# Graph layers on one core: the leading run's repair by an adding scatter, and the second graph's one-hots against numbers kept in PSUM

## The chip, the cores and the metric

The kernel runs on one core of one Trainium2 chip. The metric is the device time of one execution in microseconds. Before the change the median of three runs is 8366.63 us (8365.44 to 8374.06). The core's engines are TensorE (PE), VectorE (DVE), ScalarE (ACT), GpSimd (POOL) and SyncE (SP). They run side by side and wait for each other on semaphores. SP and ACT issue plain DMAs. POOL issues the indirect ones, which fetch or write one row for each of 128 partitions, by an index read from SBUF.

## The reference

`x` holds 12500 nodes of 256 features. A first graph has 200000 edges, sorted by target. After a layer norm, three graph layers run over it:

```python
h = x @ W
msg = h[src] * norm[:, None]
out = jax.ops.segment_sum(msg, dst, num_segments=n_nodes)
return out + b            # gelu after the first two layers
```

The result is added to `x` and normed again. It is the input of an attention over a second graph (131072 unsorted edges) that scores four experts for each node, and of four feed-forward experts that the scores mix. The second graph needs its edges sorted by target and, for each target, the number of its edges.

## The kernel before

**Running sums instead of a scatter.** The first graph's sorted edges are laid out as 128 partitions by 1564 columns, each partition holding a stretch of consecutive edges. For each column POOL issues one gather (L995, in the tail L1005) that fetches the 128 source rows of 1 KB from `feature_table` in HBM. DVE adds the row to a running sum that starts anew where the target changes (L1130, one `scalar_tensor_tensor` for each column, state in PSUM). ACT copies four columns at a time from PSUM to SBUF (L915). SP writes 16 columns at a time to `running_features_of_edges` in HBM (L1229). A batch of 16 columns lives in one of four buffers, so POOL may be up to four batches ahead of DVE. A batch is added only when all its 16 rows of gathers have landed. There are 97.75 batches in a layer. The sum of a node is then the row of its last edge, which POOL fetches at the end of the layer, 98 gathers (L1024). DVE, PE and ACT apply the weight, the bias and the gelu to these, and SP writes the table of the next layer.

**The leading run.** A node's edges may begin in one partition's stretch and end in the next's. Then the row of its last edge in the later partition lacks the earlier partition's part. PE makes these parts in one product (`carry_from` by the last columns' sums, L1042) into `ps[:, 0, 0:D]`. After all of a layer's sums are in HBM (`s_out`), POOL gathers the 128 rows at `fix_at` into `run_fix` (L1012), DVE adds PE's part to them (L1140) into `run_fixed`, and POOL writes them back to the same rows (L1016), waits for that write and starts the 98 gathers of L1024. Partitions with nothing to repair point at spare rows. This happens three times, once in each layer.

**The second graph's work is woven into layer 0.** `SecondGraph.on_vector` is a generator. In layer 0, DVE takes one step of it (up to the next `yield`) after every fourth column; 1564 columns give 391 such slots, four in a batch. First come a few preparing steps, then the 64 steps that build one-hots, then some 167 steps of a bitonic sort (exchanges at L202 and L203, sign flips at L239, transposes on PE between them), then some 20 of bookkeeping. Steps left over after the last column run at the layer's end (`for _ in between: pass`).

A one-hot step `h` builds, for 16 edges of each partition, `lo` (128 numbers by 16 edges, L377) and `hi` (98 by 16, L379): the low seven bits and the upper bits of the target, compared with the numbers 0 to 127. The numbers stand in `iota_rep` in SBUF, each repeated 16 times, in bf16. Both are `tensor_tensor` with all operands in SBUF in bf16, in one slot. PE multiplies `lo` by `hi`, 16 matmuls (L195) into `ps[:, 5, 0:98]`, which counts each node's edges. The tiles are double-buffered (`s_hot`, `s_used`). In layer 0 the running sums use PSUM banks 0 to 3, the count bank 5, and the sort's transposes banks 4 to 7, after the count.

After the layers come the attention's 1024 gathers (L1454) beside the experts' matmuls (L1539, L1550), and the mix.

Of the kernel before, what the change touches and what calls it, by code (L numbers as in the profile page):

```python
# [5 lines left out]
ALU = mybir.AluOpType  # L6
# [6 lines left out]
P = 128  # L13
U = 16
# [22 lines left out]
def build(nc, x, src, dst, gnn_w, gnn_b, w_gat, att_src, att_dst, b_gat, ln_gamma, ln_beta,  # L37
          ew1, eb1, ew2, eb2, edges2, out):
    N, D = x.shape
    NB = -(-N // P)  # L40
# [24 lines left out]
    sums_dram = nc.dram_tensor("running_features_of_edges", (E1P + 2 * P, D), F32).ap()  # L65
# [5 lines left out]
    with ExitStack() as ctx:  # L71
        def sb(name, shape, dt=F32):
            return ctx.enter_context(nc.sbuf_tensor(name, shape, dt))
# [3 lines left out]
        def sem(name):  # L77
            s = nc.alloc_semaphore(name=name)
            phase_sems.append(s)
            return s  # L80
# [12 lines left out]
        ps = ctx.enter_context(nc.psum_tensor("ps", [P, 8, 512], F32))  # L93
# [12 lines left out]
        fix_at = sb("row_of_leading_run", [P, 1], I32)  # L106
# [56 lines left out]
        iota_rep = work[:, 0:P * U // 2].bitcast(BF16).rearrange("p (m u) -> p m u", u=U)  # L163
# [3 lines left out]
        def hot_tiles(rows):  # L167

            lo = [hot_bf[0:rows, a].rearrange("p (m u) -> p m u", u=U) for a in range(2)]
            hi = [hot_bf[0:rows, 2 + a, 0:NB * U].rearrange("p (m u) -> p m u", u=U) for a in range(2)]  # L170
            return lo, hi
# [116 lines left out]
        class SecondGraph:  # L288
# [56 lines left out]
            def on_vector(self, dve):  # L345

                C = COLS2
                link = Chain(dve, self.s_d)
# [20 lines left out]
                yield  # L369
                link(nc.vector.tensor_scalar(self.keys[0].bitcast(I32), src_i, KEY_BASE, None, ALU.bitwise_or))  # L370
                lo, hi = hot_tiles(P)
                dve.sem_inc(self.s_used, 2)
                for h in range(C // U):
                    yield
                    dve.wait_ge(self.s_used, h + 1)
                    at = slice(h * U, (h + 1) * U)
                    nc.vector.tensor_tensor(lo[h % 2], iota_rep[0:P],  # L377
                                            lo16[:, at].unsqueeze(1).broadcast_to([P, P, U]), ALU.is_equal)
                    nc.vector.tensor_tensor(hi[h % 2], iota_rep[0:P, 0:NB],  # L379
                                            hi16[:, at].unsqueeze(1).broadcast_to([P, NB, U]),  # L380
                                            ALU.is_equal).then_inc(self.s_hot, 1)
                yield
# [454 lines left out]
        state = [ps[:, k // 2, (k % 2) * D:(k % 2 + 1) * D] for k in range(U)]  # L837
        spare = onehot[:].rearrange("p a u m -> p (a u m)")
        selfs = spare[:, 0:4 * 2 * D].rearrange("p (r a f) -> p r a f", r=4, a=2)
        run_fix, run_fixed = spare[:, 8 * D:9 * D], spare[:, 9 * D:10 * D]  # L840
        sums_rows = sums_dram[0:E1P].rearrange("(p c) f -> p c f", p=P)

        pairs4 = [work[:, j * 8 * D:(j + 1) * 8 * D].rearrange("p (r a f) -> p r a f", r=4, a=2) for j in range(4)]
# [17 lines left out]

        s_row = [ctx.enter_context(nc.semaphore(f"rows_in{r}")) for r in range(4)]
        s_sums = [ctx.enter_context(nc.semaphore(f"node_sums_in{r}")) for r in range(4)]
        s_fixin, s_fixout = ctx.enter_context(nc.semaphore("gnn_fix_rows_in")), ctx.enter_context(nc.semaphore("gnn_fix_rows_out"))

        def layer(l, s_stored=None):

# [13 lines left out]
            s_carry, s_fixd = sem("carries" + n_), sem("fix_done" + n_)  # L881
# [102 lines left out]
            def on_gpsimd(pool):  # L984
                pool.sem_inc(s_c, 4 * U)
                if s_stored is not None:
                    pool.wait_ge(s_stored, 16 * PAIRS)

                def gather(m, r):
                    pool.wait_ge(s_stg, m + 1)  # L990
                    pool.sem_inc(s_tick, 1)
                    pool.wait_ge(s_c, m * U + (U + 1))
                    pool.sem_inc(s_tick, 1)
                    for k in range(U):
                        nc.gpsimd.indirect_dma_start(  # L995
                            out=rows_in[r][:, k], out_offset=None, in_=table,
                            in_offset=bass.IndirectOffsetOnAxis(ap=staged[:, r, k:k + 1], axis=0),
                        ).then_inc(s_row[r], 16)
                with pool.Fori(0, LAPS) as g:
                    for r in range(4):  # L1000
                        gather(g * 4 + r, r)
                for m, r, uses, size, c in tails:
                    pool.wait_ge(s_c, m * U + (U + 1))
                    for k in range(size):
                        nc.gpsimd.indirect_dma_start(  # L1005
                            out=rows_in[r][:, k], out_offset=None, in_=table,
                            in_offset=bass.IndirectOffsetOnAxis(ap=idx[0][:, c + k:c + k + 1], axis=0),
                        ).then_inc(s_row[r], 16)

                for r in range(S):  # L1010
                    pool.wait_ge(s_out[r], chunks_out[r])
                nc.gpsimd.indirect_dma_start(  # L1012
                    out=run_fix, out_offset=None, in_=sums_dram,
                    in_offset=bass.IndirectOffsetOnAxis(ap=fix_at[:, 0:1], axis=0)).then_inc(s_fixin, 16)
                pool.wait_ge(s_fixd, 1)
                nc.gpsimd.indirect_dma_start(  # L1016
                    out=sums_dram, out_offset=bass.IndirectOffsetOnAxis(ap=fix_at[:, 0:1], axis=0),
                    in_=run_fixed, in_offset=None).then_inc(s_fixout, 16)
                pool.wait_ge(s_fixout, 16 * (l + 1))
                for n in range(PAIRS):  # L1020
                    if n >= 4:
                        pool.wait_ge(s_sums[n % 4], node_base[n % 4] + 32 * (n // 4))
                    for b in (2 * n, 2 * n + 1):
                        nc.gpsimd.indirect_dma_start(  # L1024
                            out=acc[:, b * D:(b + 1) * D], out_offset=None, in_=sums_dram,
                            in_offset=bass.IndirectOffsetOnAxis(ap=take1[:, b:b + 1], axis=0)).then_inc(s_sums[n % 4], 16)
                if last:
                    for n in range(PAIRS):
                        pool.wait_ge(s_hc, n + 3)
                        for b in (2 * n, 2 * n + 1):  # L1030
                            nc.gpsimd.indirect_dma_start(  # L1031
                                out=first_dram, out_offset=bass.IndirectOffsetOnAxis(ap=put_at[:, b:b + 1], axis=0),
                                in_=HG[:, b, CH:GW], in_offset=None).then_inc(s_put, 16)
# [74 lines left out]
            def on_vector(dve):  # L1108
                if last:
                    link = Chain(dve, s_lk)  # L1110
# [25 lines left out]
                for _ in between:  # L1136
                    pass
                dve.wait_ge(s_carry, 1)
                dve.wait_ge(s_fixin, 16 * (l + 1))
                nc.vector.tensor_tensor(run_fixed, ps[:, 0, 0:D], run_fix, ALU.add).then_inc(s_fixd, 1)  # L1140

                if last:
                    dve.sem_inc(s_v, 2)
# [77 lines left out]
            def on_sync(sp):  # L1221
# [65 lines left out]
                if l == 0:  # L1287
                    sp.wait_ge(second.s_z, 32)
            return (on_scalar, on_gpsimd, on_tensor, on_vector, on_sync, s_o) + ((s_go,) if last else ())

        first = layer(0)
        after = layer(1, first[5])
        with nc.Block() as block:
# [21 lines left out]
            def _(sp):  # L1315
                first[4](sp)
                after[4](sp)
        end_phase()
        on_scalar, on_gpsimd, on_tensor, on_vector, on_sync, s_x1out, s_go = layer(2)


# [16 lines left out]
        def area(*shape):  # L1338
# [83 lines left out]
        s_tail, s_tailt, s_ende, s_endt, s_fixd, s_fixe, s_fixo = (sem(c) for c in (  # L1422
            "tails_ready", "tails_turned", "ends_scores", "ends_exps", "ends_turned", "fix_scores", "fix_exps"))
# [17 lines left out]
        with nc.Block() as block:  # L1441
# [236 lines left out]
            @block.vector  # L1678
            def _(dve):
                on_vector(dve)  # L1680
                link = Chain(dve, s_c)
                dve.wait_ge(s_x1out, 16 * PAIRS)
# [258 lines left out]
```

## Time and profile before

| | us |
|---|---|
| median of the runs | 8366.63 |
| the profiled execution | 8364.74 |
| its span | 8362.9 |
| POOL busy | 6097.1 (73%) |
| DVE busy | 3651.4 (44%) |
| PE busy | 2172.5 (26%) |
| ACT busy | 1974.1 (24%) |

Busy time counts an engine's own instructions. A POOL gather is busy for about 0.95 us and followed by 0.30 us that the profile calls issue, so an engine that gathers all the time shows about 76%. Layer 0 ends at 2228.9, layer 1 at 4346.4 and layer 2 at 6473.0 (each time the start of the first gather at L1024); the rest lasts until 8362.9.

### The profile page before, as it was taken

The numbers are of one execution on the slowest core, as the hardware profiler recorded it, in microseconds if no ns is written. First come the engines' busy times: TensorE is split into PE (matmuls) and PEld (weight loads), VectorE is DVE, ScalarE is ACT, GpSimd is POOL, SyncE is SP. The second block draws the span as 40 slices with busy tenths as digits, with TensorE's granted clock in tenths as the row PEclk, the third lists the DMA queues.
The fourth block names the chain that finished last, engine by engine and source line by source line (L and its number), as shares of the span: only waits on it lengthen the run. The fifth ranks groups of instructions, "written<-read, shape, count | busy, mean of one in ns | idle before, by whom it ended". The sixth has DMA issues, their size and how long they took to land. (4 is left out here: it accounts for less than half of the span.)

```text
span 8362.9 us, 48755 instructions
## 1 busy us (share of the span) xinstructions
PE 2172.5 (26%) x10310; PEld 1843.9 (22%) x10310; DVE 3651.4 (44%) x7508; ACT 1974.1 (24%) x3168; POOL 6097.1 (73%) x6330
## 2 busy tenths in 40 slices
PE   1440000000220000000013000000000899999974
PEld 1330000000220000000013000000000788888863
DVE  5676666443444333343434434343433723322346
ACT  1111212122332222221224212121221422222222
POOL 5777777777677777777766777777776777777761
PEclk9999999999965555555557555555555999999987
DMA  5555555566666666666666666666666943323348
GB/s 168 187 191 203 205 204 204 204 210 210 231 211 208 212 205 215 205 215 206 213 217 214 215 206 214 206 212 208 210 211 214 281 109 74 81 74 74 74 121 249
DMA packets 590695, 1583.16 MB, mean 189 GB/s; under 512 B 136696, under 2 KB 377188, under 8 KB 551780
## 3 DMA queue, kind: packets, MB, share of 16 engines
q1 hardware_dynamic: 307092, 896.86, 29.4%
q0 software_dynamic: 281888, 669.59, 27.9%
q10 hardware_dynamic: 1584, 15.48, 0.5%
q14 instruction: 113, 0.93, 0.0%
q8 instruction: 18, 0.29, 0.0%
HBM read 820.50 MB, written 760.96 MB: 189 GB/s over the span
## 5 line engine op out<-in xcount | busy, mean ns | idle before, releaser
L995 POOL DMA_INDIRECT acc<-feature_table,staged_indices x4608 | 4415.7, 958 | 1466.3 <-issue 1365.3
L1130 DVE SCALAR_TENSOR_TENSOR ps<-ps,keep_within_node,acc 128x256 f32<-128x256 f32 x4692 | 2310.1, 492 | 3296.4 <-DMA acc<-feature_table,staged_indices 2770.8
L915 ACT COPY acc<-ps 128x1024 f32<-128x1024 f32 x787 | 796.9, 1013 | 3215.9 <-DVE ps L1130 3215.9
L1454 POOL DMA_INDIRECT acc<-attention_table,idx x1024 | 1009.4, 986 | 312.0 <-issue 311.7
L1042 PE MATMUL ps<-work,carry_from_partition 128*128 128x256 f32 x4 | 2.4, 713 | 3948.6 <-ACT work L915 3948.6
L1042 PEld LDWEIGHTS ps<-work,carry_from_partition 128*128 128x128 f32 x4 | 1.0, 312 | 3949.4 <-ACT work L915 3949.4
L915 ACT COPY work<-ps 128x1024 f32<-128x1024 f32 x386 | 390.7, 1012 | 1522.8 <-DVE ps L1130 1522.8
L1539 PE MATMUL ps<-work 128*128 128x256 f32 x3136 | 703.5, 380 | 9.0 <-ACT work L1602 8.7
L1550 PE MATMUL ps<-work,onehot 128*128 128x256 f32 x3136 | 702.9, 380 | 9.9 <-DMA work<-L_ffn_W_in 9.9
L1539 PEld LDWEIGHTS ps<-work 128*128 128x128 f32 x3136 | 597.2, 191 | 91.6 <-ACT work L1602 10.1
L1550 PEld LDWEIGHTS ps<-work,onehot 128*128 128x128 f32 x3136 | 596.9, 190 | 91.5 <-issue 10.0
L1602 ACT ACTIVATE work<-ps,eb_sb 128x256 f32<-128x256 f32 x784 | 307.6, 475 | 997.2 <-PE ps L1550 994.5
L1695 DVE TENSOR_TENSOR acc<-ps,acc 128x512 f32<-128x512 f32 x196 | 135.6, 692 | 910.5 <-PE ps L1539 910.1
L1024 POOL DMA_INDIRECT acc<-unning_features_of_edges,last_edge_of_gnn_node x294 | 292.7, 996 | 93.8 <-issue 88.7
L195 PE MATMUL ps<-onehot 128*128 128x98 bf16 x1120 | 219.4, 366 | 201.1 <-DVE onehot L379 197.5
L283 PE MATMUL ps<-ident,work 128*128 128x128 f32 x112 | 27.6, 427 | 782.7 <-DVEq L253 782.7
L195 PEld LDWEIGHTS ps<-onehot 128*128 128x128 bf16 x1120 | 158.9, 148 | 261.4 <-DVE onehot L379 222.2
L283 PEld LDWEIGHTS ps<-ident,work 128*128 128x128 f32 x112 | 21.9, 223 | 788.1 <-DVEq L253 788.1
L1102 PE MATMUL ps<-gw_sb,work 128*128 128x256 f32 x784 | 189.6, 386 | 0.0
L1042 PE MATMUL ps<-acc,carry_from_partition 128*128 128x256 f32 x2 | 1.2, 712 | 695.5 <-ACT acc L915 695.5
L1042 PEld LDWEIGHTS ps<-acc,carry_from_partition 128*128 128x128 f32 x2 | 0.5, 313 | 695.8 <-ACT acc L915 695.8
L1102 PEld LDWEIGHTS ps<-gw_sb,work 128*128 128x128 f32 x784 | 143.7, 193 | 18.0 <-issue 0.7
(366 smaller groups left out, 2989.9 us busy)
## 6 DMA issues: line engine op xcount, KB each, us to landing
unning_features_of_edges<-acc SPq DMA_DIRECT2D x195, 2048.0 KB, 7.7
unning_features_of_edges<-work SPq DMA_DIRECT2D x96, 2048.0 KB, 7.7
acc<-feature_table,staged_indices POOLq DMA_INDIRECT x4608, 2.8
expert_rows<-acc SPq DMA_DIRECT2D x196, 256.0 KB, 2.3
onehot<-feature_table SPq DMA_DIRECT2D x147, 256.0 KB, 4.4
feature_table<-acc SPq DMA_DIRECT2D x98, 256.0 KB
work<-expert_rows SPq DMA_DIRECT2D x22, 1024.0 KB, 7.8
acc<-expert_rows SPq DMA_DIRECT2D x17, 1024.0 KB, 6.9
```

The lines of the kernel that those rows point to most:

```text
L195: mm = nc.tensor.matmul(to, lo[a][:, :, k], hi[a][:, :, k], start=False, stop=False)
L283: mm = nc.tensor.transpose(flat[side][:, j * P:(j + 1) * P], a[:, j * P:(j + 1) * P], ident[:])
L915: nc.scalar.copy(sums_out[slot][:, 4 * j:4 * j + w].rearrange("p c f -> p (c f)"), ps[:, b:b + 2].rearrange("p a f -> p (a f)")[:, 0:w * D ...
L995: nc.gpsimd.indirect_dma_start(out=rows_in[r][:, k], out_offset=None, in_=table, in_offset=bass.IndirectOffsetOnAxis(ap=staged[:, r, k:k + ...
L1024: nc.gpsimd.indirect_dma_start(out=acc[:, b * D:(b + 1) * D], out_offset=None, in_=sums_dram, in_offset=bass.IndirectOffsetOnAxis(ap=take1 ...
L1102: mm = nc.tensor.matmul(ps[:, 4 + r, a * D:(a + 1) * D], zt[:, r, a, k * P:(k + 1) * P], gw_sb[:, l, k], start=(k == 0), stop=(k == KD - 1 ...
L1130: nc.vector.scalar_tensor_tensor(state[k % HELD], state[(k - 1) % HELD if k else before], keep1[:, c + k:c + k + 1], rows_in[r][:, k], ALU ...
L1454: nc.gpsimd.indirect_dma_start(out=rows[:, i % 2, c], out_offset=None, in_=gat_table, in_offset=bass.IndirectOffsetOnAxis(ap=idx[1][:, sta ...
L1539: mm = nc.tensor.matmul(to, hid[:, x % 2, m, a * P:(a + 1) * P], w2[:, x, m], start=(m == 0), stop=(m == KH - 1), skip_group_check=True)
L1550: mm = nc.tensor.matmul(ps[:, 2 * (x % 2) + m // 2, (m % 2) * 2 * P:(m % 2 + 1) * 2 * P], w1[:, x, k, m * P:(m + 1) * P], xt[:, r, :, k], ...
L1602: ge = nc.scalar.activation(hid[:, x % 2, m], ps[:, 2 * (x % 2) + m // 2, (m % 2) * 2 * P:(m % 2 + 1) * 2 * P], ACT.Gelu, bias=b1[:, x, m: ...
L1695: nc.vector.tensor_tensor(yst[:, x], ps[:, 4 + x % 2].rearrange("p (a f) -> p a f", a=2), yst[:, x], ALU.add).then_inc(s_yc, 1)
```

## The change

Two edits are made together.

In each layer's repair, the gather of the 128 rows (L1012), its semaphore and its SBUF tile `run_fix` are gone. DVE no longer adds but copies PE's part from PSUM to `run_fixed`. POOL's scatter carries `compute_op=ALU.add`, so that the DMA adds the rows to those in HBM.

In the one-hots, DVE first copies one set of the 128 numbers from `iota_rep` to `ps[:, 6, 0:128]` in f32, in a slot of its own. `lo` and `hi` are compared with this PSUM row, read with each number repeated 16 times, instead of with `iota_rep`. A `yield` is put between `lo` and `hi`, so each has its own slot: 128 slots for the one-hots instead of 64, and one for the copy.

```diff
--- before.py
+++ after.py
@@ -369,14 +369,18 @@
                 yield
                 link(nc.vector.tensor_scalar(self.keys[0].bitcast(I32), src_i, KEY_BASE, None, ALU.bitwise_or))
                 lo, hi = hot_tiles(P)
+                iota_ps = ps[:, 6, 0:P]
+                yield
+                link(nc.vector.tensor_copy(iota_ps, iota_rep[:, :, 0]))
                 dve.sem_inc(self.s_used, 2)
                 for h in range(C // U):
                     yield
                     dve.wait_ge(self.s_used, h + 1)
                     at = slice(h * U, (h + 1) * U)
-                    nc.vector.tensor_tensor(lo[h % 2], iota_rep[0:P],
+                    nc.vector.tensor_tensor(lo[h % 2], iota_ps.unsqueeze(2).broadcast_to([P, P, U]),
                                             lo16[:, at].unsqueeze(1).broadcast_to([P, P, U]), ALU.is_equal)
-                    nc.vector.tensor_tensor(hi[h % 2], iota_rep[0:P, 0:NB],
+                    yield
+                    nc.vector.tensor_tensor(hi[h % 2], iota_ps[:, 0:NB].unsqueeze(2).broadcast_to([P, NB, U]),
                                             hi16[:, at].unsqueeze(1).broadcast_to([P, NB, U]),
                                             ALU.is_equal).then_inc(self.s_hot, 1)
                 yield
@@ -837,7 +841,7 @@
         state = [ps[:, k // 2, (k % 2) * D:(k % 2 + 1) * D] for k in range(U)]
         spare = onehot[:].rearrange("p a u m -> p (a u m)")
         selfs = spare[:, 0:4 * 2 * D].rearrange("p (r a f) -> p r a f", r=4, a=2)
-        run_fix, run_fixed = spare[:, 8 * D:9 * D], spare[:, 9 * D:10 * D]
+        run_fixed = spare[:, 9 * D:10 * D]
         sums_rows = sums_dram[0:E1P].rearrange("(p c) f -> p c f", p=P)
 
         pairs4 = [work[:, j * 8 * D:(j + 1) * 8 * D].rearrange("p (r a f) -> p r a f", r=4, a=2) for j in range(4)]
@@ -861,7 +865,7 @@
 
         s_row = [ctx.enter_context(nc.semaphore(f"rows_in{r}")) for r in range(4)]
         s_sums = [ctx.enter_context(nc.semaphore(f"node_sums_in{r}")) for r in range(4)]
-        s_fixin, s_fixout = ctx.enter_context(nc.semaphore("gnn_fix_rows_in")), ctx.enter_context(nc.semaphore("gnn_fix_rows_out"))
+        s_fixout = ctx.enter_context(nc.semaphore("gnn_fix_rows_out"))
 
         def layer(l, s_stored=None):
 
@@ -1009,13 +1013,10 @@
 
                 for r in range(S):
                     pool.wait_ge(s_out[r], chunks_out[r])
-                nc.gpsimd.indirect_dma_start(
-                    out=run_fix, out_offset=None, in_=sums_dram,
-                    in_offset=bass.IndirectOffsetOnAxis(ap=fix_at[:, 0:1], axis=0)).then_inc(s_fixin, 16)
                 pool.wait_ge(s_fixd, 1)
                 nc.gpsimd.indirect_dma_start(
                     out=sums_dram, out_offset=bass.IndirectOffsetOnAxis(ap=fix_at[:, 0:1], axis=0),
-                    in_=run_fixed, in_offset=None).then_inc(s_fixout, 16)
+                    in_=run_fixed, in_offset=None, compute_op=ALU.add).then_inc(s_fixout, 16)
                 pool.wait_ge(s_fixout, 16 * (l + 1))
                 for n in range(PAIRS):
                     if n >= 4:
@@ -1136,8 +1137,7 @@
                 for _ in between:
                     pass
                 dve.wait_ge(s_carry, 1)
-                dve.wait_ge(s_fixin, 16 * (l + 1))
-                nc.vector.tensor_tensor(run_fixed, ps[:, 0, 0:D], run_fix, ALU.add).then_inc(s_fixd, 1)
+                nc.vector.tensor_copy(run_fixed, ps[:, 0, 0:D]).then_inc(s_fixd, 1)
 
                 if last:
                     dve.sem_inc(s_v, 2)
```

## Rows read from the trace of the kernel before

**Rows 1.** The page: shares of the chain that ended last, by engine and by line.

```profile
POOL 31%; issue 10%; DVE 2%; PE 1%; DMA 1%; ACT 0%; POOLq 0%; SPq 0%; DVEq 0%; ACTq 0%
```

**Rows 2.** Windows of L995's gathers, layer 0: stretch, length, busy (count), clock, DMA share, GB/s.

```profile
245.50:591.30 345.80, 267.75 (x256) 1.00 0.57 195
591.30:1541.30 950.00, 726.54 (x734) 1.00 0.59 202
1541.30:2195.90 654.60, 478.40 (x506) 1.00 0.61 209
```

**Rows 3.** Timeline, POOL, hot stage: start, length, instruction, count, idle before it.

```profile
411.32 1.79 POOL L995 DMA_INDIRECT acc<-feature_table,staged_indices  x1 [0.30 <-issue]
...
415.91 1.19 POOL L995 DMA_INDIRECT acc<-feature_table,staged_indices  x1 [0.30 <-issue]
```

**Rows 4.** Timeline, DVE, the same stretch.

```profile
411.07 1.21 DVE L377 TENSOR_TENSOR onehot<-work,HG 128x2048 bf16<-128x2048 bf16 x1
412.20 0.97 DVE L379 TENSOR_TENSOR onehot<-work,HG 128x1568 bf16<-128x1568 bf16 x1
413.09 2.07 DVE L1130 SCALAR_TENSOR_TENSOR ps<-ps,keep_within_node,acc 128x256 f32<-128x256 f32 x4
415.06 1.21 DVE L377 TENSOR_TENSOR onehot<-work,HG 128x2048 bf16<-128x2048 bf16 x1
```

**Rows 5.** Timelines, end of layer 0: one POOL gather, then the DVE rows around it.

```profile
2241.40 0.95 POOL L1024 DMA_INDIRECT acc<-unning_features_of_edges,last_edge_of_gnn_node  x1 [0.30 <-issue]
...
2240.49 0.69 DVE L1206 TENSOR_TENSOR work<-acc,onehot 128x512 f32<-128x512 f32 x1 [1.82 <-DMA acc<-unning_features_of_edges,last_edge_of_gnn_node]
2241.10 0.87 DVE L1213 SCALAR_TENSOR_TENSOR work<-ps,dinv,gb_sb 128x256 f32<-128x256 f32 x2
```

**Rows 6.** Instructions of L1130 and of L995, 1600 to 2100: duration min/median/max.

```profile
L1130 DVE SCALAR_TENSOR_TENSOR ps<-ps,keep_within_node,acc x401: 491/493/494, 1599.8 to 2099.9; 128x256 f32<-128x256 f32 x134
...
L995 POOL DMA_INDIRECT acc<-feature_table,staged_indices x400: 942/946/956, 1600.2 to 2099.0; - x134
```

**Rows 7.** Durations of L1140 and of L1695, min/median/max in ns.

```profile
L1140 DVE TENSOR_TENSOR onehot<-ps,onehot x3: 423/425/425, 2225.5 to 6469.6; 128x256 f32<-128x256 f32 x3
...
L1695 DVE TENSOR_TENSOR acc<-ps,acc x196: 690/692/693, 6738.7 to 8094.8; 128x512 f32<-128x512 f32 x196
```

**Rows 8.** Timeline, DVE: last instruction of the second graph, then layer 0's last columns.

```profile
1540.85 0.32 DVE L461 CAST first_edge_of_node<-work 128x98 int32<-128x98 f32 x1
...
2195.43 8.61 DVE L1130 SCALAR_TENSOR_TENSOR ps<-ps,keep_within_node,acc 128x256 f32<-128x256 f32 x16 [11.37 <-DMA acc<-feature_table,idx]
```

**Rows 9.** Timeline, end of layer 0: the leading runs repaired.

```profile
2217.71 1.22 PE L1042 MATMUL ps<-acc,carry_from_partition 128*128 128x256 f32 x2 [695.54 <-ACT acc L915]
...
2222.19 0.94 POOL L1012 DMA_INDIRECT onehot<-unning_features_of_edges,row_of_leading_run  x1 [13.56 <-DMA unning_features_of_edges<-acc]
2225.47 0.42 DVE L1140 TENSOR_TENSOR onehot<-ps,onehot 128x256 f32<-128x256 f32 x1 [8.86 <-DMA onehot<-unning_features_of_edges,row_of_leading_run]
2226.18 1.00 POOL L1016 DMA_INDIRECT unning_features_of_edges<-onehot,row_of_leading_run  x1 [3.04 <-DVE onehot L1140]
2228.88 0.97 POOL L1024 DMA_INDIRECT acc<-unning_features_of_edges,last_edge_of_gnn_node  x1 [1.70 <-DMA unning_features_of_edges<-onehot,row_of_leading_run]
```

**Rows 10.** Timeline, POOL, end of layer 1.

```profile
4340.07 0.95 POOL L1012 DMA_INDIRECT onehot<-unning_features_of_edges,row_of_leading_run  x1 [14.15 <-DMA unning_features_of_edges<-work]
4343.71 1.00 POOL L1016 DMA_INDIRECT unning_features_of_edges<-onehot,row_of_leading_run  x1 [2.69 <-DVE onehot L1140]
```

**Rows 11.** Timeline, POOL, end of layer 2.

```profile
6463.97 0.94 POOL L1012 DMA_INDIRECT onehot<-unning_features_of_edges,row_of_leading_run  x1 [13.64 <-DMA unning_features_of_edges<-work]
6470.30 1.00 POOL L1016 DMA_INDIRECT unning_features_of_edges<-onehot,row_of_leading_run  x1 [5.38 <-DVE onehot L1140]
```

**Rows 12.** Landing of L1012 and of L1016, us from issue, min/median/max.

```profile
DMA to landing us min/median/max: 2.8/3.2/5.5
...
DMA to landing us min/median/max: 2.4/2.4/2.4
```

## The prediction

> **What bounds the kernel now.** I read the chain of waits first: POOL's instructions and the idle time called issue make up most of the chain outside the experts' matmuls [rows 1]. So I looked at POOL by stretches of layer 0. The reader is to see that there the same gathers come in three prices [rows 2]. After the second graph's work has ended, one gather is busy 478.40 / 506 = 0.945 us. While the one-hots are built it is 267.75 / 256 = 1.046, and in the sort 726.54 / 734 = 0.990. To each comes 0.30 us of issue. In all three POOL never stops, so each tenth of a microsecond that a gather loses is lost to the end: layer 0 ends when its 1564 gathers have ended.
>
> The timelines show where the tenth goes [rows 3, 4]. L377 runs from 411.07 to 412.28. The gather that starts at 411.32 takes 1.79 us, 0.84 more than 0.95. L377 again runs from 415.06 to 416.27, and the gather of 415.91 takes 1.19, 0.24 more. Both are explained by one reading: a gather needs something 0.13 us after its start (411.45, 416.03), which L377 holds until its own end. The rows with a PSUM input don't hold it. L1213 reads PSUM and one SBUF tile, writes SBUF, and runs over the moment 2241.53 of the gather that starts at 2241.40, which takes 0.95 [rows 5]. L1130 runs 401 times beside 400 gathers whose longest is 956 ns [rows 6].
>
> **The one-hots.** Removed: the holding by 64 L377 and 64 L379. That is 256 x (1.046 - 0.945) = 25.7 us of POOL's time in the hot stage. It is on the path as a whole, since POOL is what layer 0 waits for; neither DVE (busy with a batch for less than POOL needs, below) nor the DMA engines (share 0.57) is next. I count it in full, because L1213 and L1130 cost the gathers nothing. Bounds: all of it, or none; the row of the same kind (PSUM and SBUF in, SBUF out) stands next to the first.
>
> Beside a measured row stands a rule: the Trainium skill, page "SBUF — State Buffer", section "Who interferes with whom", says that a DVE instruction with two SBUF inputs contends with a GpSimd instruction that reads SBUF, while one with at most one SBUF input, outside the two-port modes, doesn't. By it the hot stage's 25.7 us go altogether. For `lo` and `hi` themselves no row here shows it.
>
> Added: DVE time. With f32 from PSUM the compare can't be expected at L377's 0.59 ns per element. L1140 takes 425 ns for 256 elements and L1695 692 for 512, both `tensor_tensor` with one PSUM operand [rows 7]: 1.043 ns per element over 158 ns. So `lo` (2048) takes 2.29 us for 1.21, `hi` (1568) 1.79 for 0.97. A batch has 16 columns, 8.61 us [rows 8], and now two `lo` and two `hi`: 8.61 + 2 x 4.08 = 16.8 us. Before it was 8.61 + 4 x 2.02 = 16.7 (L377's start to the next L1130's, [rows 4]). POOL needs 16 x 1.249 = 19.98 us for a batch, so DVE stays under it by 3.2 us: cost nothing. That cover is gone when `lo` and `hi` together pass (19.98 - 8.61) / 2 = 5.7 us.
>
> Moved: everything of the second graph behind the one-hots, by 65 slots (64 of the new `yield`, one of the copy to PSUM, a small DVE instruction). A slot is four columns, 4 x 1.249 = 5.0 us, so 325 us. The second graph's last instruction stands at 1541, layer 0's last full batch starts on DVE at 2195 [rows 8]: between them lie 506 gathers [rows 2], some 126 slots. The end comes near 1541 - 26 + 325 = 1840, before the layer's. Nothing waits for it earlier, so cost nothing; PE's 16 matmuls for each pair only get more time. The sort keeps its loss, 734 x 0.045 = 33 us. It moves by 16 batches and one slot, and the first slot of a batch holds a gather longer than the others, as in the hot stage; this may turn out 3 us either way, and I take 0.
>
> **The repair.** Removed: L1012, its landing, L1140 and the way back to POOL. From L1012's start to L1016's it is 2226.18 - 2222.19 = 3.99 us in layer 0, 3.64 in layer 1, 6.33 in layer 2 [rows 9 to 11]: 13.96 in all, with nothing beside it on POOL, and the 98 gathers of L1024 behind it. The wait on DVE that remains is not late: PE's part is there at 2218.93, the copy needs some 0.4 us, POOL gets free at 2222.19.
>
> Added: the scatter must read what it adds to. L1016 lands 2.4 us after its issue, L1012 after 2.8 to 5.5 [rows 12]. At the least the addition costs nothing (the same bytes leave); at the most a read in full ahead of the write, 2.8 us. No row shows an adding DMA; I take the middle, 1.4 us, three times: 4.2. Then the scatter stands where the gather stood: in layer 2 SP has just queued loads and the gather needed 5.5 instead of 2.8, so 2.7 more there, and 0.4 in layer 0 (its landing 3.2). Sum of the repair: 13.96 - 4.2 - 3.1 = 6.7 us, with ends at 2.5 and 14.
>
> On the price of that read there is only a page: the Trainium skill, "DMA: Bandwidth & Descriptors", section "Latency and other measured facts", gives HBM's access as 0.2 us on average and 2 at high load. By it the three additions would cost an estimated 0.6 to 6 us and the repair would give 4.9 to 10.3. No run here shows it.
>
> **Sum.** 25.7 + 6.7 = 32.4 us less than the profiled execution's 8364.74, so 8332.3. The median of the runs lies 1.9 above that execution, so 8334 as a median. After layer 0 everything only starts earlier; the experts' stage is bound by PE and does not see it.
>
> **Rivals.**
>
> *The repair gives nothing or costs.* The adding scatter may land much later, say 7 us later than a plain one in each layer. For it: no row of such a DMA, and it reads and writes the same 128 rows. Against it: 128 KB only. Then 13.96 - 3.1 - 21 = -10 us, and 8366.6 - 25.7 + 10 = 8351. Chance 0.10, together with a small gain from only part of the one-hots.
>
> *The port is held just as before, only longer (slower).* Place: the one-hot slots of layer 0. If the compare with PSUM still holds what the gather needs, each of the 128 instructions catches one gather and keeps it for its length less half of POOL's 1.25 us period: 64 x (2.29 - 0.62) + 64 x (1.79 - 0.62) = 182 us, for the 25.7 of before, so 156 more, less 6.7: 8516. It decides from the point where a caught gather waits on average 32 / 128 = 0.25 us. For it: `lo` and `hi` write bf16 by a broadcast read, which L1213 and L1130 don't. Against it: [rows 5, 6]. Chance 0.04.
>
> *DVE becomes the bound of layer 0 (slower).* If the repeated read from PSUM beside a bf16 operand ran at twice the 1.043 ns, `lo` and `hi` would take 4.4 and 3.4 us, a batch 24.3 us of DVE. That is 4.3 us too much in each of 32 batches, 138 in all. POOL's lead of some two batches (40 us) takes up part: 98 - 32 = 66 slower, 8433. It decides when the overrun passes 40 + 32 us, which is `lo` + `hi` above 6.8 us. For it: no row of this form. Against it: all rows of one PSUM operand agree on 1.04. Chance 0.05.
>
> *The one-hots' gain is hidden anyway.* Only the repair counts: 8360. For it would speak a second engine at its limit in the hot stage; DVE is at 16.8 of 19.98 and no wait of POOL on it is in [rows 3]. Chance 0.04.
>
> **How the numbers follow.** Forecast 0.77, rivals 0.23. A change under 0.2% (17 us) can't be told from none with this kernel. The forecast's own range is 8325 to 8346: the repair between 2.5 and 14, the sort's 3 us, and some spread of the runs (8365.4 to 8374.1 before). The 8-in-10 range reaches a little into the first rival: 8323 to 8350. Faster by over 0.2% is under 8350: 0.83 (the forecast, and half of the first rival, rounded up). Within: 0.07. Slower: 0.10, the two slow rivals and what I haven't thought of.
>
> **What would show it.** In the profile after, L995's gathers in the hot stage, which is then some 640 us long, have a mean of 0.945 and no 1.79 or 1.19. `lo` and `hi` take near 2.29 and 1.79, and the batch of DVE ends before the next one's rows land. The second graph's last instruction stands near 1840. L1024's first gather follows the scatter's start by 2.7 to 5.5 us in layers 0 and 1, where it now follows L1012's by 6.7. Layer 0 ends some 28 us earlier, layers 1 and 2 each 2 us more. A hot stage with gathers over 1 us, a DVE that never idles in it, or second-graph steps after the last column would make the prediction wrong.

## The result, and the profile after

The changed kernel takes 8334.0 us (median of 7 runs, 8327.7 to 8345.2), the kernel before 8366.6 (7 runs, 8359.1 to 8374.1). The ratio is 0.9961, with a 95% interval of 0.9951 to 0.9971. Timed again later it was 8332.8 against 8368.0, ratio 0.9955 (0.9941 to 0.9968). The forecast was 8334. The interval of the kernel with the repair alone, below, leaves out one slow execution of 10981.5 us.

The profiled execution of the changed kernel has a span of 8338.8 us. First the windows of the edge gathers in layer 0, to be held against [rows 2]: stretch, its length, busy (count), clock, DMA share, GB/s. The first is the one-hots' stage, the second the sort and the bookkeeping, the third the rest.

```profile
247.90:888.90 641.00, 484.74 (x513) 1.00 0.61 210
888.90:1838.40 949.50, 725.91 (x735) 1.00 0.59 202
1838.40:2170.00 331.60, 234.33 (x248) 1.00 0.61 208
```

The reader is to see that a gather of the hot stage now costs 484.74 / 513 = 0.945 us, where it was 1.046, although the stage is nearly twice as long. Its 513 gathers have a longest of 0.958. The middle stretch is what it was: 725.91 / 735 = 0.988. From layer 0's first edge gather to its last it is 1987.2 us instead of 2013.0: 25.8 less.

The DVE instructions that replaced L377 and L379 (duration min/median/max in ns), with the copy to PSUM ahead of them:

```profile
L374 DVE CAST ps<-work x1: 378/378/378, 245.3 to 245.3; 128x128 f32<-128x128 bf16 x1
...
L380 DVE TENSOR_TENSOR onehot<-ps,HG x64: 2280/2281/2282, 247.9 to 882.9; 128x2048 bf16<-128x2048 f32 x64
...
L383 DVE TENSOR_TENSOR onehot<-ps,HG x64: 1779/1780/1782, 259.2 to 887.1; 128x1568 bf16<-128x1568 f32 x64
```

And the last instruction of the second graph, to [rows 8]:

```profile
1838.17 0.21 DVE L465 CAST first_edge_of_node<-work 128x98 int32<-128x98 f32 x1
```

It stands at 1838, 297 later than before, and layer 0's columns go on for 350 us after it.

The repair at the end of layer 0, to [rows 9]:

```profile
2193.46 0.42 DVE L1140 COPY onehot<-ps 128x256 f32<-128x256 f32 x1 [2.35 <-PE ps L1043]
2196.70 1.64 POOL L1017 DMA_INDIRECT unning_features_of_edges<-onehot,row_of_leading_run  x1 [13.75 <-DMA unning_features_of_edges<-acc]
2201.01 0.99 POOL L1025 DMA_INDIRECT acc<-unning_features_of_edges,last_edge_of_gnn_node  x1 [2.67 <-DMA unning_features_of_edges<-onehot,row_of_leading_run]
```

and of layer 2, to [rows 11]:

```profile
6435.36 1.62 POOL L1017 DMA_INDIRECT unning_features_of_edges<-onehot,row_of_leading_run  x1 [13.55 <-issue]
6441.97 0.98 POOL L1025 DMA_INDIRECT acc<-unning_features_of_edges,last_edge_of_gnn_node  x1 [4.99 <-DMA unning_features_of_edges<-onehot,row_of_leading_run]
```

and the landing of its scatter in the three layers, to [rows 12]:

```profile
DMA to landing us min/median/max: 3.8/4.0/6.3
```

DVE's copy is done at 2193.88, long before POOL is free at 2196.70. The scatter itself takes POOL 1.64 us instead of 1.00, and lands after 3.8 to 6.3 us instead of 2.4. From a layer's last edge gather to its first node gather it was 21.19, 21.44 and 23.62 us; it is 19.01, 18.72 and 21.11. That is 2.18, 2.72 and 2.51 less, 7.4 in all. The second profile of the same kernel has 10.3 less in all, so this distance varies from one execution to the next: it begins with the wait for the last sums to land in HBM. Counted only from the moment when they have landed and POOL starts the repair, the three repairs took 22.1 us before and take 15.0, in the second profile 14.1: 7.1 to 8.0 less.

### The profile page after: what moved, and what is told of

It is laid out like the page before. It is cut to its first block and busy times, and to the rows that moved or that the text cites. A ratio compares the mean times of both kernels' runs of the same rounds, so it can differ in the third digit from the quotient of the medians.

```text
span 8338.8 us, 48748 instructions
## 1 busy us (share of the span) xinstructions
PE 2177.7 (26%) x10310; PEld 1847.7 (22%) x10310; DVE 3769.8 (45%) x7509; ACT 1973.4 (24%) x3168; POOL 6071.0 (73%) x6327
## 5 line engine op out<-in xcount | busy, mean ns | idle before, releaser
L1454 POOL DMA_INDIRECT acc<-attention_table,idx x1024 | 1007.6, 984 | 312.1 <-issue 312.1
L1695 DVE TENSOR_TENSOR acc<-ps,acc 128x512 f32<-128x512 f32 x196 | 135.6, 692 | 912.4 <-PE ps L1539 912.3
L195 PE MATMUL ps<-onehot 128*128 128x98 bf16 x1120 | 219.5, 366 | 499.9 <-DVE onehot L383 496.3
L195 PEld LDWEIGHTS ps<-onehot 128*128 128x128 bf16 x1120 | 159.0, 148 | 560.1 <-DVE onehot L383 521.1
L380 DVE TENSOR_TENSOR onehot<-ps,HG 128x2048 bf16<-128x2048 f32 x64 | 146.0, 2281 | 0.0
L1693 DVE TENSOR_TENSOR acc<-acc,work 128x512 f32<-128x512 f32 x196 | 133.7, 682 | 22.9 <-DMA acc<-x_after_gnn 20.1
```

Of the source, the lines that this page charges most:

```text
L195: mm = nc.tensor.matmul(to, lo[a][:, :, k], hi[a][:, :, k], start=False, stop=False)
L380: nc.vector.tensor_tensor(lo[h % 2], iota_ps.unsqueeze(2).broadcast_to([P, P, U]), lo16[:, at].unsqueeze(1).broadcast_to([P, P, U]), ALU.i ...
L1454: nc.gpsimd.indirect_dma_start(out=rows[:, i % 2, c], out_offset=None, in_=gat_table, in_offset=bass.IndirectOffsetOnAxis(ap=idx[1][:, sta ...
L1695: nc.vector.tensor_tensor(yst[:, x], ps[:, 4 + x % 2].rearrange("p (a f) -> p a f", a=2), yst[:, x], ALU.add).then_inc(s_yc, 1)
```

## The experiments

"Lengthening" below is what the edge gathers of a stretch are busy beyond 0.9455 us each.

**One part alone: the repair.** The kernel before with the second half of the diff.

> Only the repair is changed (adding scatter, no gather); the one-hots stay as before. Theory: the repair and the one-hots add up, each in its own place. From the start of the scatter to the first gather of node rows as after the change (4.31, 4.03 and 6.61 us in layers 0, 1, 2), so 2.2 to 2.7 us less in each layer between the last edge gather and the first node gather: 7.4 us less than before in all, time about 8359. The hot stage keeps its 25.7 us of lengthened gathers. Rival (the repair gives nothing, the one-hots everything): 8366, and the three distances 21.2, 21.4 and 23.6 us as before.

Measured: 8359.5 us (11 runs) against 8366.6, ratio 0.9989 (0.9979 to 0.9998): the gain is only just clear of none. The three distances are 19.08, 19.35 and 20.41 us, 7.4 less in all, as in the first profile after the change; from POOL's start of the repair it is 7.8 less. Layer 2's first node gather stands only 2.4 us earlier than before in this profile (6470.6 for 6473.0); the edge gathers of each layer took some 1.5 us longer in it. The hot stage's lengthening is 25.8 us, as before. The scatter in all three layers:

```profile
L1013 POOL DMA_INDIRECT unning_features_of_edges<-onehot,row_of_leading_run x3: 1617/1626/1641, 2224.1 to 6464.9; - x3
```

**One part alone: the one-hots.** The changed kernel with the old repair.

> Only the one-hots are changed (PSUM numbers, lo and hi in slots of their own); the repair is as before. Theory: every gather of the hot stage takes 0.945 us, layer 0's 1564 gathers 25.7 us less, time about 8341. Rival (the two edits overlap, for instance the later second graph slows something else): less than 20 us.

Measured: 8343.3 us (8 runs, 8336.3 to 8352.8), ratio 0.9971 (0.9961 to 0.9982). Lengthening in the hot stage 0.5 us; layer 0's edge gathers 1987.6 us from first to last, 25.4 less than before. The two parts give 7.1 and 23.3 us, 30.4 together; the whole change gives 32.6 and, the second time, 35.2. They add up within the spread of the runs. The old repair's three distances are 22.1, 22.3 and 23.4 us in this profile, 1.5 more in all than in the profile before: that much they vary with nothing changed in them.

**Only the operand's memory.** The numbers are f32 in both kernels, in SBUF here:

```diff
-                iota_ps = ps[:, 6, 0:P]
+                iota_ps = iota[:]
                 yield
-                link(nc.vector.tensor_copy(iota_ps, iota_rep[:, :, 0]))
```

> As after the change, but the numbers that the one-hots are compared with are f32 in SBUF instead of f32 in PSUM: the same DVE durations (about 2.28 and 1.78 us) and the same 128 slots, only the memory of one operand differs. Theory (the gather needs something that a DVE instruction with two SBUF inputs holds): nearly each of the 128 instructions catches a gather for 1 to 1.6 us; the hot stage's gathers are lengthened by 130 to 200 us in all, time about 8334 + 160 = 8490. Rival (it is DVE's two-at-a-time bf16 mode that holds the gather, not where the operand lies): nothing is lengthened, time about 8334.

Measured: 8522.3 us (2 runs), ratio 1.0187 (1.0169 to 1.0206). The windows row of the gathers in its hot stage:

```profile
247.80:1073.40 825.60, 670.26 (x511) 1.00 0.47 162
```

That is 1.31 us a gather, a lengthening of 187 us, within the 130 to 200 expected. Its `lo` and `hi` take the same 2.28 and 1.78 us as from PSUM. DVE's timeline:

```profile
398.48 1.78 DVE L382 TENSOR_TENSOR onehot<-iota,HG 128x1568 bf16<-128x1568 f32 x1
...
402.15 2.28 DVE L379 TENSOR_TENSOR onehot<-iota,HG 128x2048 bf16<-128x2048 f32 x1
```

POOL's beside it:

```profile
398.96 2.12 POOL L998 DMA_INDIRECT acc<-feature_table,staged_indices  x1 [0.30 <-issue]
...
402.63 2.62 POOL L998 DMA_INDIRECT acc<-feature_table,staged_indices  x1 [0.30 <-issue]
```

The reader is to see that both gathers end 0.82 us after the DVE instruction they met: L382 ends at 400.26 and the gather at 401.08, L379 at 404.43 and the gather at 405.25. A free gather has 0.82 us left 0.13 after its start. So the gather asks at 0.13 us and gets what it needs when the instruction ends. All 128 compares of this hot stage hold a gather, and each such gather ends 0.81 to 0.83 us after its compare. The 0.13 is worked out from these ends: in the sort of the changed kernel, L202s that start 0.09 to 0.10 us after a gather, two SBUF inputs each, lengthen it by 0.01 us at most. The rival, that only the two-at-a-time bf16 rate held it, falls: these compares run at the full-width rate of 1.04 ns an element and hold it all the longer. The trace agrees with the Trainium skill's page "SBUF — State Buffer", section "Who interferes with whom": a DVE instruction with two SBUF inputs contends with a GpSimd instruction that reads SBUF, one with at most one SBUF input, outside the two-port modes, doesn't, and the shared port pair is an exclusive lock.

The trace of the kernel before shows both sides of this as well. Fourteen gathers ask while L210 or L211 of the sort runs, a `tensor_tensor` with one input in PSUM and one in SBUF; none takes over 0.95 us. One of them, DVE's row and then POOL's:

```profile
885.98 0.68 DVE L211 TENSOR_TENSOR work<-ps,work 128x512 f32<-128x512 f32 x1
...
886.08 0.95 POOL L995 DMA_INDIRECT acc<-feature_table,staged_indices  x1 [0.30 <-issue]
```

But a single SBUF input isn't always harmless. L251 multiplies 1024 f32 numbers in SBUF by a scalar in 0.74 us, so faster than 1.04 ns an element:

```profile
1102.46 0.74 DVE L251 TENSOR_SCALAR work<-work 128x1024 f32<-128x1024 f32 x1
...
1102.66 1.36 POOL L995 DMA_INDIRECT acc<-feature_table,staged_indices  x1 [0.30 <-issue]
```

This gather too ends 0.82 us after the DVE instruction. And where an L251 starts 0.25 us after a gather, so after the moment of asking, the gather still takes 1.11 us: for this kind of instruction 0.13 us isn't the only moment that counts.

**Only the added yield.** The compares read `iota_rep` in SBUF in bf16, as before, in slots of their own.

> As after the change, but the one-hots are compared with the bf16 numbers in SBUF as before: only the added yield is left, lo and hi in slots of their own. Theory (two SBUF inputs hold the gather): no relief; the first instruction of a batch catches a gather for 0.8 us and the others for 0.2 to 0.7, in 32 batches instead of 16: the excess goes from 25.7 to 40 to 57 us, time about 8334 + 50 = 8384. Rival (the relief comes from the two no longer standing back to back): excess under 10 us, time about 8340.

Measured: 8404.9 us (2 runs), ratio 1.0047 (1.0028 to 1.0065). The gathers of its hot stage:

```profile
248.60:954.50 705.90, 550.57 (x511) 1.00 0.55 190
```

1.077 us each, a lengthening of 67 us, more than the 40 to 57 expected. The kernel is 38 us slower than before although it has the new repair; against the kernel with the new repair alone (8359.5) the yield costs 45. In the shared slot, `hi` ran while the gather held up by `lo` was already served; in its own it catches one, as DVE's and POOL's timelines show:

```profile
415.91 0.96 DVE L381 TENSOR_TENSOR onehot<-work,HG 128x1568 bf16<-128x1568 bf16 x1
...
416.11 1.58 POOL L997 DMA_INDIRECT acc<-feature_table,staged_indices  x1 [0.30 <-issue]
```

The gain comes from PSUM, not from the yield. That the yield is needed to make room for the slower compares is argued from DVE's time in a batch; no run settles it on a chip where the kernel before takes 8367 us.

**Four variants of the change.** They ran on a chip on which the kernel before takes 10711.4 us; what differs there is told under the last of them.

Both compares from PSUM in one slot (the added `yield` removed):

> As after the change, but without the yield between lo and hi: both f32-from-PSUM compares in one slot, 64 slots instead of 128. A batch of DVE then takes 8.6 + 4 x 3.9 = 24.2 us against POOL's 20.0, in 16 batches: 67 us over. Theory (POOL's lead over DVE of about two batches, 40 us, is used up first): no gather is lengthened by holding, but POOL waits for DVE's running sums in the last batches of the hot stage, some 25 to 30 us in all, time about 8362. Rival (the yield has no part in the gain, the lead hides all of it): 8334. Rival (no lead): 8400.

Measured: 10719.9 us, ratio 1.0005 (0.9994 to 1.0015). Between longer stops a batch takes DVE 23.5 us in its hot stage, and POOL waits some 3.8 us for it in most batches, so here DVE is the bound. But there are stops of DVE of up to 30 us on that chip as well (below), and what the yield is worth without them stays open.

A plain scatter for the adding one:

```diff
-                    in_=run_fixed, in_offset=None, compute_op=ALU.add).then_inc(s_fixout, 16)
+                    in_=run_fixed, in_offset=None).then_inc(s_fixout, 16)
```

> As after the change, with a plain scatter in the repair instead of the adding one; it leaves out the addition of the rows that are in HBM. It prices the addition. Theory (the addition costs in POOL's own instruction, 1.62 us against 1.00, and in landing, 4.0 against 2.4): from the scatter's start to the first node gather 2.7 us in layers 0 and 1 instead of 4.31 and 4.03. In layer 2, if SP's loads ahead of it are what made 6.61, some 4 to 5; if the addition alone made it, 2.7.

Measured, one run of 10756.6 us: scatter to first node gather 3.82, 3.60 and 4.15 us, where the adding scatter has 4.33, 4.09 and 6.30 in the variant before it, on the same chip. Duration on POOL, and landing:

```profile
L1017 POOL DMA_INDIRECT unning_features_of_edges<-onehot,row_of_leading_run x3: 1001/1004/1005, 2587.8 to 7463.8; - x3
...
DMA to landing us min/median/max: 3.3/3.6/3.9
```

The addition costs POOL 0.62 us in its instruction, and 0.5 us of the distance in layers 0 and 1 (0.5 to 0.9 if the other adding kernels on that chip are taken). In layer 2 it costs 2.2: there the plain scatter is hardly later for SP's loads, the adding one is. The expectation of 2.7 us in layers 0 and 1 failed. Whether that chip, or the scatter's new place right behind the last sums, makes a plain one land after 3.3 to 3.9 us instead of 2.4 isn't told apart.

SP's loads of layer 2 after the repair:

```diff
                     for r in range(S):
                         sp.wait_ge(s_out[r], chunks_out[r])
+                    sp.wait_ge(s_fixout, 16 * (l + 1))
```

> As after the change, but in layer 2 SP issues its loads of own rows and of x only after the repair's scatter has landed. Theory (the scatter of layer 2 stands behind these eight loads): scatter to first node gather falls from 6.61 to about 4.1 us; the first addition of own rows then waits for its load instead, some 3 to 4 us later than now relative to the gather, which later gathers make good or not: time 8334 less 0 to 2.5. Rival (the longer landing is of another cause): 6.6 as before.

Measured: 10753.1 us, ratio 1.0037 (1.0026 to 1.0048). Layer 2's repair in the one-slot variant, with the loads ahead:

```profile
7424.02 1.62 POOL L1016 DMA_INDIRECT unning_features_of_edges<-onehot,row_of_leading_run  x1 [30.52 <-issue]
7430.32 0.98 POOL L1024 DMA_INDIRECT acc<-unning_features_of_edges,last_edge_of_gnn_node  x1 [4.68 <-DMA unning_features_of_edges<-onehot,row_of_leading_run]
```

and here, with the loads behind:

```profile
7477.26 1.62 POOL L1017 DMA_INDIRECT unning_features_of_edges<-onehot,row_of_leading_run  x1 [30.52 <-issue]
7481.34 0.98 POOL L1025 DMA_INDIRECT acc<-unning_features_of_edges,last_edge_of_gnn_node  x1 [2.45 <-DMA unning_features_of_edges<-onehot,row_of_leading_run]
```

6.30 us against 4.08: the loads are the cause of the late landing.

Fillers before the sort's steps:

```diff
                         if k % 4 == 3:
+                            if l == 0 and second.sorting:
+                                n = 343 if k == 3 else 449
+                                nc.vector.tensor_reduce(gates[:, 0, 0:1], keep1[:, 0:n], AX.X, ALU.max)
                             next(between, None)
```

> As after the change, and before each of the sort's steps in layer 0 DVE does a filler, one maximum over 343 (first slot of a batch) or 449 (other slots) columns of keep_within_node, one SBUF input, 0.5 or 0.6 us. Theory (a gather asks 0.13 us after its start, once in 1.25 us, and waits only where an instruction with two SBUF inputs is running at that moment): the fillers move the steps' 1.29 us to just behind an asking gather, so that the next asks near the step's end. The sort stage's lengthening of gathers falls from 32.4 us to 8 to 20, time about 8334 - 18 = 8316, though DVE does more. Rival (the lengthening grows with DVE's load or its use of SBUF ports as such): 32 us or more, time 8334 or above.

Measured: 10776.3 us, ratio 1.0063 (1.0046 to 1.0079). Lengthening in the sort stage 22.1 us, against 30.7 and 31.5 in the two variants above with the same slots.

Two more ran on a third chip, where the kernel before takes 10690.5.

> The fillers before the sort's steps and the loads after layer 2's repair, both on top of the change. On the last chip the fillers took the sort stage's lengthening to 22 us (others there 31) and the late loads took layer 2's scatter to first node gather from 6.3 to 4.1. Theory: both hold on a chip where the kernel before takes 8366: sort stage 8 to 20 us instead of 32.4, layer 2's distance 4.1 instead of 6.6 of which the first addition may take back a part; time 8334 - 12 to - 22, about 8317. Rival (the fillers help only where DVE's waits are long): 32 us in the sort stage and 8332.

Measured: 10739.4 us, ratio 1.0048 (1.0034 to 1.0062); sort stage 25.7 us, layer 2's distance 4.21.

> lo and hi from PSUM in one slot, as before on the other chip, here for a chip where a column takes DVE 0.54 us. A batch of DVE takes 24.2 us against POOL's 20.0 in 16 batches, 67 us over. Theory (a lead of two batches, 40 us, is used up first): 25 to 30 us of waits on POOL in the hot stage, time about 8362. Rival (the lead hides all): 8334. Rival (no lead): 8400.

Measured: 10666.4 us, ratio 0.9983 (0.9972 to 0.9994).

What differs on these two chips shows in the waits of the hot stage (waiting engine and line, releaser, us in total, times, longest). The variant with the late loads, 260 to 1150 us:

```profile
DVE onehot L380 <- remote: 315.1, 19, 29.6
POOL acc L999 <- DVE ps L1131: 191.8, 13, 19.9
```

The changed kernel on a chip where before takes 8368, same stretch:

```profile
POOL acc L999 <- DVE ps L1131: 5.5, 18, 0.3
```

DVE stands still for up to 29.6 us, released by something the profile calls remote, and POOL waits 191.8 us for DVE's running sums instead of 5.5. The kernel tells more: all that L380 waits for is `s_used`, which only PE's last matmul of each 16 (L195) counts up. PE's and DVE's timelines at one stop:

```profile
358.76 3.15 PE L195 MATMUL ps<-onehot 128*128 128x98 bf16 x16 [11.67 <-DVE onehot L383]
...
392.23 2.29 DVE L380 TENSOR_TENSOR onehot<-ps,HG 128x2048 bf16<-128x2048 f32 x1 [29.60 <-remote]
```

The record of the sixteenth matmul ends at 361.9, and the count comes at 392.2. In the second profile of the changed kernel, where before takes 8368, the count comes 0.01 us after that end each time. So DVE waits for PE here, whose matmul or signal comes up to 30 us late. In layers 1 and 2 the edge gathers come at one in 1.38 us, not 1.25; some of them take 1.80 us, with no instruction of two SBUF inputs beside them. There DVE's stops bound layer 0, POOL's relief brings little, and the variants with 128 slots lose 0.4 to 0.6%. What makes PE late, and why one slot does better than two, is open, and so is whether it belongs to the chip; the unmodified change wasn't run on such a chip.

**The change once more, and with fillers and late loads.**

> The changed kernel itself again. Where the kernel before takes about 8366, DVE idles in each batch and the change gives 32 us: 8334. Where it takes about 10700, the last six kernels showed DVE standing still for up to 27 us at a time with POOL waiting for its running sums; theory there: DVE bounds layer 0, the longer compares are paid in full and the change costs 20 to 60 us against before. Rival there: DVE's stops are independent of the compares and the change gives its 30 us.

Measured: 8332.8 us (5 runs, 8325.5 to 8333.0) against 8368.0.

> The change with fillers before the sort's steps and the loads after layer 2's repair. Where before takes about 8366: the sort stage's lengthening 8 to 20 us instead of 32.4, layer 2's scatter to first gather 4.1 instead of 6.6, time 12 to 22 us under the changed kernel. Where before takes about 10700: within 15 us of the changed kernel, since POOL isn't the bound of layer 0.

Measured: 8323.7 us (5 runs, 8319.5 to 8325.9), ratio to before 0.9946 (0.9933 to 0.9960): 9 us under the changed kernel, whose own five on the same chip overlap it by one value. It is the fastest version. The windows row of the sort stage in the changed kernel:

```profile
888.70:1838.40 949.70, 726.10 (x734) 1.00 0.59 202
```

and with fillers:

```profile
889.80:1838.40 948.60, 721.67 (x746) 1.00 0.60 205
```

Lengthening 32.1 and 16.3 us, in stretches of the same length. DVE's timeline in it:

```profile
1294.96 0.61 DVE L1140 TENSOR_REDUCE gates<-keep_within_node 128x1 f32<-128x449 f32 x1
1295.48 0.68 DVE L202 TENSOR_TENSOR work<-work 128x512 f32<-128x512 f32 x1
1296.08 0.68 DVE L203 TENSOR_TENSOR work<-work 128x512 f32<-128x512 f32 x1
```

and POOL's:

```profile
1295.31 0.94 POOL L1002 DMA_INDIRECT acc<-feature_table,staged_indices  x1 [0.30 <-issue]
1296.56 1.03 POOL L1002 DMA_INDIRECT acc<-feature_table,staged_indices  x1 [0.30 <-issue]
```

Beside the filler, which has one SBUF input, the gather of 1295.31 takes 0.94 us. The filler puts the exchange at 1295.48, behind that gather's moment of asking, 1295.44. The next asks at 1296.69 and waits only for the end of L203, 0.08 us. DVE does 167 instructions more and POOL gets faster: it isn't DVE's load that lengthens a gather, but where an instruction lies when the gather asks. Layer 2's distance fell from 5.85 to 4.04 us, but its 98 node gathers took 128.4 us from first to last instead of 125.3, so from layer 2's last edge gather to its last node gather the late loads give 0.9 us; why these gathers slow down wasn't tried. Layer 0's edge gathers took 1973.2 us instead of 1988.6, 15.4 less, of which the medians show 9. In the two profiles the last attention gather starts 22.0 us earlier and the last stage is 12.6 longer (it varies, see below); with five runs each the rest isn't settled.

## Why the prediction was right

**The one-hots, 25.7 us.** Layer 0's edge gathers gave 25.8 in the changed kernel and 25.4 alone. The reading that a gather asks 0.13 us after its start, and that a PSUM operand lets it through, was the step that the sum stood on, and the kernel with f32 in SBUF shows it by itself: the same compares, one operand moved, 187 us. The second rival had put such compares at 182 us if they held the gathers, so its price was right too; its condition isn't met with the numbers in PSUM.

**DVE's cover.** `lo` and `hi` came at 2.281 and 1.780 us for 2.29 and 1.79 forecast. What DVE keeps idle in a batch shows in its waits for rows in the hot stage (us in total, times, longest):

```profile
DVE ps L1131 <- DMA acc<-feature_table,staged_indices: 137.7, 32, 7.0
```

That is 4.3 us a batch, for 3.2 forecast, since a batch takes DVE 15.8 us and not 16.8. POOL's 18 waits for DVE, 5.5 us in all, are 0.3 us each, no longer than its usual issue. The prediction didn't say that this cover can fail for a reason outside the compares: on two chips DVE was the bound of layer 0, as in its third rival, by another cause than the one named there.

**The moved work.** 1838 for 1840 forecast; the sort's lengthening stayed at 31 to 32 us.

**The repair, 6.7 us.** Measured 7.4 by the distances, alone and together, though they vary by some 3 us between executions (10.3 in the second profile); 7.1 to 8.0 by the repair itself; 7.1 by the medians of the repair alone. The price of the addition was put at 1.4 us for a read ahead of the write. From scatter to first node gather it is 4.31 and 4.03 us in layers 0 and 1 for 2.70 before, so 1.6 and 1.3, and 3.9 in layer 2, where 1.4 + 2.7 was forecast. The sum was right, but partly by luck: 1.4 was the middle between none and a full read. What it is made of was not seen: 0.62 us lies in POOL's own instruction, and against a plain scatter in the same place the addition costs 0.5 us in layers 0 and 1, on another chip. Whether the rest is that chip or the new place isn't told. The trace doesn't contradict the 0.2 to 2 us that the Trainium skill gives for HBM's access ("DMA: Bandwidth & Descriptors", "Latency and other measured facts"), but no run isolates that read.

**What follows.** Layer 0 ended 27.9 us earlier, as forecast (28). Layer 1 ended 27.8 and layer 2 31.0 earlier, where 30 and 32 would follow from the forecast: from layer 0's first node gather to layer 1's first edge gather this execution took 2.7 us longer than the one before the change. In the profiled execution the last attention gather (L1454) starts 31.7 us earlier than before, the end comes only 24.1 earlier. That isn't the change: from that gather to the end it is 322.3 us in this execution and 309.3 in the second profile of the same kernel. The last stage varies by 13 us from one execution to the next; the medians give the 32 us back in full. That the median falls on the forecast to the microsecond is luck: its seven runs lie up to 17.6 us apart.

## What to carry to other kernels

Where GpSimd issues gathers without pause, look for gathers of two lengths, and at which DVE instruction lies 0.13 us after the start of the long ones: two SBUF inputs cost the gather the rest of that instruction, and moving one input to PSUM ends it even at half of DVE's speed, as long as DVE keeps idle time in each batch. Where the operand can't be moved, a filler that shifts the instruction behind the asking gather took at best half of the loss. The filler here was a `tensor_reduce`; a fast one-input instruction like L251's `tensor_scalar` would hold gathers itself. A gather, an addition and a scatter of the same rows can become one adding scatter, here for 2 to 3 us each.

## What the runs showed of the hardware

- An adding indirect scatter of 128 rows of 1 KB takes POOL 1.62 us against 1.00 for a plain one. Behind SP's queued loads of 256 KB the gather that follows it starts 6.30 us after it instead of 4.08; behind a plain scatter with the same loads it was 4.15.
- The same kernel takes 8367 or 8368 us on two chips and 10690 to 10711 on two others. There the signal of a finished matmul came up to 30 us late, and DVE stopped for it. Variants of a change that gives 0.4% on the first were between 0.2% faster and 0.6% slower on the others.
